# Router of a fuzzy-attention stage on one Trainium2 core: chunks of four batches at the start and of two at the end, shorter lags, late factors on VectorE

## The chip, the cores and the metric

The kernel runs on one core of a Trainium2 chip. The metric is the device time of one execution in microseconds (us), the median of the runs shown. Lower is better.

## What is computed

A two-layer audio model on 32 sequences of 255 tokens with 128 features. The stages are, in order: signature features of the input (L0_tok), fuzzy attention (L0_attn), a top-1 mixture of 8 experts (L0_ffn), relative attention, and a top-2 mixture of 64 experts. The change lies in the fuzzy-attention stage, which also prepares the top-1 experts. Cut to what matters:

```python
# fuzzy attention, added to h
x = layernorm(h)
p = softmax(q @ k.T)
h = h + max(min(p / 0.3, (1 - p) / 0.3), 0) @ x
# top-1 experts: which expert each token goes to
y = layernorm(h)
logits = y @ Wr + br
expert = argmax(logits)          # top_k with k = 1
h = h + ffn[expert](y)
```

## The kernel before, in words

One function, `fuzzy_attention`, holds the stage. Each engine (SyncE, VectorE, ScalarE, GpSimd, TensorE) has its own program, written out by hand as a loop over steps `b`. A step of an engine does pieces of work for batches at fixed offsets from `b`; on VectorE for example the maxima of batch b+2, the membership of b+1, the rows of b+4, the factors of b+2 and then the add of batch b (line 809: the attention result is added to `h`; lines 811 to 813: its statistics). Every engine executes its program strictly in that order, and the engines wait for each other on semaphores that count (`score_done`, `out_done`, `h_ready` and so on). A batch is two tiles of 128 tokens.

Beside the attention runs the router of the next stage. It works on chunks of `G` = 4 batches (`CT` = 8 tiles), N = 8 chunks. For a chunk c:

- **factors** (GpSimd, `factors0`, lines 1018 to 1042): from the batches' statistics the reciprocal deviation `rstd0` and the shift `shift0`, 22 chained small instructions. They wait for the last batch's statistics. GpSimd's program is factors of c, then the sends of chunk c-2, for c = 0 to 9. The last chunk's factors are on VectorE with a square root on ScalarE (`last_factors`, lines 904 to 920; line 1009).
- **normalise** (VectorE, `normalised`, line 824): the chunk's tiles into `y`, in halves of four tiles, at steps 4c+5 and 4c+6.
- **turn rows** (TensorE, `turn_rows`, line 1121) at steps 4c+6 and 4c+8, behind that step's other work, and ScalarE's copy to `yT` (`read_rows`, line 996) at 4c+7 and 4c+9.
- **route** (TensorE, line 1131): the logits, at step 4c+10, and **choose** (VectorE, lines 830 to 852): the expert of each token, at the end of the same step. It gives `both_ready`.
- **count** (TensorE, lines 1142 to 1149) at step 4c+11, ahead of the attention result of that step (line 1112): it needs `both_ready`. **Locate** (VectorE, lines 859 to 870): each token's place in the slots; it gives `at_ready`.
- **send** (GpSimd, line 1053): one indirect DMA per tile scatters the normalised rows to `x_slots` in HBM. Before the sends of tiles 3 and 6 it waits for `out_done` of a later batch.

The chunk N-2 is routed at step 32, after the last batch, with the last chunk behind it. At the end TensorE forms the total count (line 1155), and VectorE's `plan` (lines 873 to 902) writes the table of padding places (line 876) and the tables of the expert stage. SyncE then writes eight blocks of padding rows (lines 758 to 766), each after reading its place from the table. The next stage, `experts_top1`, waits on SyncE for all sends and all padding writes (lines 1239 and 1240) and then loads tiles of `x_slots` (line 1230). `logit_ps` and `count_ps` lie beside the attention result in the two `out_ps` buffers.

```python
for c in range(N + 2):
    if c < N - 1:
        factors0(c)
    if c > 1:
        send(c - 2)
```

Of the kernel before, what the change touches and what calls it, by code (L numbers as in the profile page):

```python
# [8 lines left out]
U32 = mybir.dt.uint32  # L9
# [5 lines left out]
P = 128  # L15
# [6 lines left out]
G = 4  # L22
# [652 lines left out]
NB0, U0, U1 = 5, 8, 8  # L675
ST0 = (B * L + E0 * (P - 1)) // P + 1
# [16 lines left out]
def fuzzy_attention(nc, K, h, mean, rstd, stats, weights, x_slots, no_token, tables, cleared, behind, sent, padded):  # L693
# [5 lines left out]
    CT = 2 * G  # L699
    N = NT // CT  # L700
# [3 lines left out]
    with Bench(nc, "fuz") as m:  # L704
        def ring(name, shape, n=2):
# [11 lines left out]
        logit_ps, count_ps = (out_ps[k][:, 0, D:D + CT * E0].rearrange("p (t e) -> p t e", e=E0) for k in range(2))  # L717
# [23 lines left out]
         total_done, pads_ready, tables_ready, tick_ready, var_ready, std_ready) = (m.sem(n) for n in (  # L741
             "stats_ready vec gp rstd_ready y_ready y_turned yT_ready logit_done both_ready count_done at_ready "
             "total_done pads_ready tables_ready tick_ready var_ready std_ready").split())
        def run(step, ahead):
            for b in range(-ahead, B + 2 * G + 4):
                step(b)
# [6 lines left out]
        def chunk(b, lag, work):  # L753

            if (b - lag) % G == 0 and 0 <= (b - lag) // G < N:
                work((b - lag) // G)

        with nc.Block(no_gpsimd_drain=True) as block:
# [10 lines left out]
            def _(dve):  # L769
# [47 lines left out]
                def normalised(c, k):  # L817

                    n = c % NB
                    dve.wait_ge(rstd_ready, c + 1)  # L820
                    if c >= NB:
                        dve.wait_ge(sent[n], 16 * CT * (c // NB))
                    for t in range(k * G, (k + 1) * G):
                        last = nc.vector.tensor_scalar(y[n][:, t, 0:D], h[:, c * CT + t, :], rstd0[c % 2][:, t:t + 1],
                                                       shift0[c % 2][:, t:t + 1], ALU.mult, ALU.add)
                    last.then_inc(y_ready, 1)

                def choose(c):

                    j = c % 2  # L830
                    rank = K["rank0"][:].unsqueeze(1).to_broadcast(wide)
                    dve.wait_ge(logit_done, c + 1)
                    link(nc.vector.tensor_tensor(logits[:], logit_ps, bias_sb[:].unsqueeze(1).to_broadcast(wide),
                                                 ALU.add))
                    link(nc.vector.tensor_reduce(best[:], logits[:], AX.X, ALU.max))
                    link(nc.vector.tensor_tensor(mask[:], logits[:], best[:].unsqueeze(2).to_broadcast(wide),
                                                 ALU.is_equal))

                    link(nc.vector.tensor_tensor(mask[:], mask[:], rank, ALU.mult))
                    link(nc.vector.tensor_reduce(first[j][:], mask[:], AX.X, ALU.max))  # L840
                    link(nc.vector.tensor_tensor(onehot[j][:], rank, first[j][:].unsqueeze(2).to_broadcast(wide),
                                                 ALU.is_equal))
# [3 lines left out]
                    nc.vector.tensor_tensor(both[j][:], onehot[j][:], K["real"][:, c * CT:(c + 1) * CT].unsqueeze(2)  # L846
                                            .to_broadcast(wide), ALU.mult).then_inc(both_ready, 1)
                    dve.wait_ge(both_ready, c + 1)
                    link(nc.vector.tensor_reduce(chunk_sum[:], both[j][:].rearrange("p t e -> p e t"), AX.X, ALU.add))
# [4 lines left out]
                def locate(c):  # L854

                    j, n = c % 2, c % NB
                    tiles = slice(c * CT, (c + 1) * CT)
                    dve.wait_ge(count_done, c + 1)
                    link(nc.vector.tensor_tensor(mask[:], onehot[j][:], count_ps, ALU.mult))
                    link(nc.vector.tensor_reduce(place[:], mask[:], AX.X, ALU.add))  # L860
                    link(nc.vector.scalar_tensor_tensor(place[:], first[j][:], -float(REGION), place[:],
                                                        ALU.mult, ALU.add))
                    link(nc.vector.scalar_tensor_tensor(place[:], place[:], float(E0 * REGION), K["real"][:, tiles],
                                                        ALU.add, ALU.mult))
                    if c >= NB:
                        dve.wait_ge(sent[n], 16 * CT * (c // NB))
                    nc.vector.tensor_tensor(at[n][:], place[:], K["pad_to"][:, tiles], ALU.add)
                    dve.wait_ge(y_ready, 2 * c + 2)
                    nc.vector.tensor_copy(y[n][:, :, ROW_AT].bitcast(U32), K["pair_row"][:, tiles])\
                        .then_inc(at_ready, 1)  # L870

                def plan(c):

                    dve.wait_ge(total_done, 1)
                    link(nc.vector.tensor_copy(counts[:], count_ps[:, 0, :]))
# [28 lines left out]
                def last_factors():  # L904

                    c = N - 1
                    mean_e, m2_e, mean_o, m2_o = (stats[:, c * CT:NT, k] for k in (1, 2, 4, 5))
                    dve.wait_ge(stats_ready, B)
                    dve.wait_ge(rstd_ready, c)
                    dve.wait_ge(y_ready, 2 * c - 2)  # L910
                    link(nc.vector.tensor_tensor(spread[:], mean_e, mean_o, ALU.subtract))
                    link(nc.vector.scalar_tensor_tensor(spread[:], spread[:], 0.25, spread[:], ALU.mult, ALU.mult))
                    link(nc.vector.tensor_tensor(var[:], m2_e, m2_o, ALU.add))
                    link(nc.vector.scalar_tensor_tensor(var[:], var[:], 1.0 / D, spread[:], ALU.mult, ALU.add))
# [100 lines left out]
            def _(pool):  # L1015
                link = Chain(pool, gp)

                def factors0(c):
# [5 lines left out]
                    if c >= 2:  # L1024
                        pool.wait_ge(y_ready, 2 * c - 2)
# [2057 lines left out]
```

## Time and profile before

| | us |
|---|---|
| Runs | 1925.25, 1920.18, 1919.71 |
| Median | 1920.18 |
| Span of the profiled execution | 1922.3 |

The page gives no time of the profiled execution apart from its span, so the span stands for both. PE is TensorE's matmuls, DVE VectorE, ACT ScalarE, POOL GpSimd, SPq SyncE's queue of DMA issues. PEclk is the clock granted to TensorE, 1.00 for 2.4 GHz and 0.50 for 1.2 GHz. In a timeline a row has the start and the length in us; `x4` means that four like instructions are merged; behind it, in brackets, stands the idle time of the engine before the row and what ended it. `fuz_`, `exp_` and `all_` name the stage of a tile (`all_h` is `h`).

### The profile page before, as it was taken

The numbers are of one execution on the slowest core, as the hardware profiler recorded it, in microseconds if no ns is written. First come the engines' busy times: TensorE is split into PE (matmuls) and PEld (weight loads), VectorE is DVE, ScalarE is ACT, GpSimd is POOL, SyncE is SP. The second block draws the span as 40 slices with busy tenths as digits, with TensorE's granted clock in tenths as the row PEclk, the third lists the DMA queues.
The fourth block names the chain that finished last, engine by engine and source line by source line (L and its number), as shares of the span: only waits on it lengthen the run. The fifth ranks groups of instructions, "written<-read, shape, count | busy, mean of one in ns | idle before, by whom it ended". The sixth has DMA issues, their size and how long they took to land. (4 is left out here: it accounts for less than half of the span.)

```text
span 1922.3 us, 59270 instructions
## 1 busy us (share of the span) xinstructions
PE 1656.3 (86%) x21927; PEld 1392.3 (72%) x21927; DVE 1402.0 (73%) x3369; ACT 938.9 (49%) x2305; POOL 882.1 (46%) x1710
## 2 busy tenths in 40 slices
PE   5999999999979884999599999999999999648750
PEld 4888888888858773999478888888888888525430
DVE  6777777877758884666787888888888888635434
ACT  2222212221228770677467777777777777424320
POOL 3333333333202566566232455445555555547771
PEclk9999999999989995999699999999999999869985
DMA  8900000000022001222323333333333333256537
GB/s 298 165 0 0 0 0 0 0 0 0 0 81 102 23 25 55 65 72 65 124 60 63 74 87 78 77 77 78 76 79 80 86 77 78 63 149 171 169 102 271
DMA packets 312667, 147.60 MB, mean 77 GB/s; under 512 B 205238, under 2 KB 291284, under 8 KB 312020
## 3 DMA queue, kind: packets, MB, share of 16 engines
q1 hardware_dynamic: 299876, 118.38, 25.3%
q0 software_dynamic: 12544, 25.91, 3.9%
q8 instruction: 157, 2.57, 0.6%
q14 instruction: 90, 0.74, 0.1%
HBM read 72.03 MB, written 73.37 MB: 76 GB/s over the span
## 5 line engine op out<-in xcount | busy, mean ns | idle before, releaser
L2143 POOL DMA_INDIRECT x_slots<-rel_x,rel_at x128 | 135.5, 1059 | 212.5 <-PE rel_s_ps L1727 186.9
L535 PE MATMUL tok_main_ps<-tok_w_h,tok_feat_h 128*128 128x512 f32 x512 | 205.3, 401 | 0.9 <-DVE tok_feat_low L99 0.9
L1966 ACT ACTIVATE rel_e<-rel_s_ps,rel_neg_max 128x255 f32<-128x255 f32 x512 | 200.2, 482 | 10.7 <-DVE rel_neg_max L2299 9.5
L535 PE MATMUL tok_main_ps<-tok_w_h,tok_feat_l 128*128 128x512 f32 x512 | 200.6, 392 | 0.0
L535 PE MATMUL tok_main_ps<-tok_w_l,tok_feat_h 128*128 128x512 f32 x512 | 200.3, 391 | 0.0
L2299 DVE TENSOR_REDUCE rel_neg_max<-rel_s_ps 128x4 f32<-128x1020 f32 x128 | 155.9, 1218 | 53.2 <-PE rel_s_ps L1727 51.2
L84 POOL TENSOR_TENSOR tok_q_pre<-tok_v_q,tok_v 128x128 f32 (+1 forms) x32 | 39.0, 1219 | 310.5 <-DVE tok_q L274 295.8
L1707 PE MATMUL rel_s_ps<-rel_k_h,rel_q_head_h 128*128 128x256 f32 x512 | 154.6, 302 | 0.2 <-DVE rel_q_head_l L2273 0.2
L1748 PE MATMUL rel_t_ps<-all_k_ident,rel_e 128*128 128x128 f32 x1024 | 139.3, 279 | 14.4 <-issue 14.0
L294 DVE TENSOR_TENSOR tok_prod<-tok_main_ps,tok_v 128x1024 f32<-128x1024 f32 x64 | 78.4, 1225 | 97.9 <-PE tok_main_ps L540 97.9
L1748 PEld LDWEIGHTS rel_t_ps<-all_k_ident,rel_e 128*128 128x128 f32 x1024 | 109.6, 141 | 47.0 <-issue 45.8
L1707 PE MATMUL rel_s_ps<-rel_k_l,rel_q_head_h 128*128 128x256 f32 x512 | 143.5, 280 | 0.0
L1707 PE MATMUL rel_s_ps<-rel_k_h,rel_q_head_l 128*128 128x256 f32 x512 | 143.2, 280 | 0.0
L2661 POOL DMA_INDIRECT y_rows<-exp_y,exp_x x128 | 123.4, 964 | 34.7 <-issue 33.8
L301 DVE TENSOR_REDUCE tok_inc<-tok_prod 128x128 f32<-128x1024 f32 x64 | 128.1, 2002 | 2.2
L435 ACT ACTIVATE tok_r2v_h<-tok_r2v 128x1024 fp32r<-128x1024 f32 x32 | 33.9, 1061 | 191.6 <-DVE tok_r2v L84 191.6
L1762 PE MATMUL rel_t_ps<-attn_value_table,rel_eT 128*32 128x64 f32 x6656 | 119.5, 221 | 0.8 <-DVE rel_eT L2307 0.7
L1762 PEld LDWEIGHTS rel_t_ps<-attn_value_table,rel_eT 128*32 128x32 f32 x6656 | 98.9, 110 | 24.7 <-issue 20.8
L445 ACT ACTIVATE tok_feat_h<-tok_a_ps 128x512 fp32r<-128x512 f32 x64 | 38.3, 598 | 156.8 <-PE tok_a_ps L521 136.4
L1975 ACT ACTIVATE rel_eT<-rel_t_ps 128x512 f32<-128x512 f32 x128 | 76.5, 598 | 74.9 <-PE rel_t_ps L1748 74.8
L535 PEld LDWEIGHTS tok_main_ps<-tok_w_h,tok_feat_l 128*128 128x128 f32 x512 | 96.5, 189 | 21.0
L535 PEld LDWEIGHTS tok_main_ps<-tok_w_h,tok_feat_h 128*128 128x128 f32 x512 | 97.0, 189 | 19.2 <-DVE tok_feat_low L99 1.0
(406 smaller groups left out, 4725.2 us busy)
## 6 DMA issues: line engine op xcount, KB each, us to landing
rel_q_rep<-q_rows SPq DMA_DIRECT2D x256, 64.0 KB, 2.5
o_rows<-rel_rv SPq DMA_DIRECT2D x256, 64.0 KB
x_slots<-early_zeros SPq DMA_DIRECT2D x16, 520.0 KB, 6.2
exp_x<-x_slots SPq DMA_DIRECT2D x32, 260.0 KB, 3.0
y_rows<-early_zeros SPq DMA_DIRECT2D x16, 512.0 KB, 5.8
final_y<-y_rows SPq DMA_DIRECT2D x16, 512.0 KB, 12.0
exp_x<-x_slots SPq DMA_DIRECT2D x72, 65.0 KB, 1.9
q_rows<-rel_qT SPq DMA_DIRECT2D x64, 64.0 KB
```

Of the source, the lines that this page charges most:

```text
L84: return nc_eng.tensor_tensor(out, left.unsqueeze(3).to_broadcast([P, n, a, c]), right.unsqueeze(2).to_broadcast([P, n, a, c]), ALU.mult)
L294: nc.vector.tensor_tensor(prod[:, s], main_ps[s][:].rearrange("p (c o) -> p c o", c=C), vt[:, bass.ds(2 * b + s, 1), :].rearrange("p n c - ...
L301: nc.vector.tensor_reduce(inc[:, s, :], prod[:, s].rearrange("p c o -> p o c"), AX.X, ALU.add).then_inc(inc_ready, 1)
L535: nc.tensor.matmul(main_ps[s][:, cols], feat[fk][:, s, j, :], w_p[wk][:, j, cols], start=(j == 0 and (fk, wk) == (0, 0)), stop=False)
L1707: nc.tensor.matmul(s_ps[u % 2][:, n, :], q_head[r][qk][:, 4 * blk:4 * blk + 4].rearrange("p c h i -> p (c h i)"), keys_for(k_p[r][kk], u), ...
L1748: last = nc.tensor.transpose(t_ps[:, t, n, :], e[u % 2][:, n, t * P:(t + 1) * P], ident[:])
L1762: last = nc.tensor.matmul(rv_ps[32 * c:32 * c + 32, n, :], eT[s][:, t, blk % (NBLK // 2), 32 * c:32 * c + 32], vtab[:, w:w + QUAD, :].rear ...
L1966: last = nc.scalar.activation(e[u % 2][:, n, 0:L], s_ps[u % 2][:, n, 0:L], ACT.Exp, bias=neg_max[u % 2][:, n:n + 1])
L1975: nc.scalar.activation(eT[s][:, 0, n:n + UB], t_ps[:, 0], ACT.Copy).then_inc(eT_a, 1)
L2143: nc.gpsimd.indirect_dma_start(x1_slots[:], bass.IndirectOffsetOnAxis(ap=at[n][:, k, t:t + 1], axis=0), x1[n][:, t, k, :], None).then_inc( ...
L2299: nc.vector.tensor_reduce(neg_max[u % 2][:], s_ps[u % 2][:, :, 0:L], AX.X, ALU.max, negate=True)\
L2661: nc.gpsimd.indirect_dma_start(y1_rows[:], bass.IndirectOffsetOnAxis(ap=x[j][:, t, ROW_AT:ROW_AT + 1].bitcast(U32), axis=0), y[j][:, t, :] ...
```

## The change

The chunks get sizes of their own: six of four batches and four of two. The pieces of a chunk are placed by functions of the chunk: normalise at `rows_at`, which is the last batch's step + 2 (for chunks 0 to 6) or + 1 (7 to 9); the turned rows one step after it, one half per step, now ahead of route, count and result; route two or three steps after `rows_at`, locate one more. Factors of chunks 7 to 9 move to VectorE, with a Newton iteration in place of ScalarE's square root. The guards of the sends come two batches earlier. `logit_ps` and `count_ps` move to the buffer that belongs to their step.

```diff
+SIZES0 = (4,) * 6 + (2,) * 4
+FIRSTS0 = tuple(sum(SIZES0[:c]) for c in range(len(SIZES0)))
+ON_POOL0 = 7
+def sent_before(c, j=None):
+    j = c % NB0 if j is None else j
+    return 16 * sum(2 * SIZES0[k] for k in range(c) if k % NB0 == j)
...
-            for b in range(-ahead, B + 2 * G + 4):
+            for b in range(-ahead, B + G + 1):
...
-        def chunk(b, lag, work):
-            if (b - lag) % G == 0 and 0 <= (b - lag) // G < N:
-                work((b - lag) // G)
+        def halves(c):
+            return 2 * SIZES0[c] // G
+        def half(c, k=0):
+            return sum(halves(j) for j in range(c)) + k
+        def last_of(c):
+            return FIRSTS0[c] + SIZES0[c] - 1
+        def tiles_of(c):
+            return slice(2 * FIRSTS0[c], 2 * (FIRSTS0[c] + SIZES0[c]))
+        def rows_at(c, k=0):
+            return last_of(c) + (2 if c < ON_POOL0 else 1) + k
+        def route_at(c):
+            return rows_at(c) + 1 + halves(c)
+        def at_step(b, when, work):
+            for c in range(N):
+                if when(c) == b:
+                    work(c)
+        def half_at_step(b, lag, work):
+            for c in range(N):
+                for k in range(halves(c)):
+                    if rows_at(c, k) + lag == b:
+                        work(c, k)
+        def beside(b, s, c):
+            return out_ps[b % 2][:, s, D:D + 2 * SIZES0[c] * E0].rearrange("p (t e) -> p t e", e=E0)
+        def logit_ps(c):
+            return beside(route_at(c), 0, c)
+        def count_ps(c):
+            return beside(route_at(c) + 1, 1, c)
...
-                def last_factors():
-                    c = N - 1
...
+                def late_factors(c):
+                    j, k = c % 2, 2 * SIZES0[c]
...
+                    dve.wait_ge(stats_ready, last_of(c) + 1)
                     dve.wait_ge(rstd_ready, c)
...
+                    dve.wait_ge(y_ready, half(c - 1))
+                    link(nc.vector.tensor_tensor(center_c, mean_e, mean_o, ALU.add))
+                    link(nc.vector.tensor_tensor(spread_c, mean_e, mean_o, ALU.subtract))
+                    link(nc.vector.scalar_tensor_tensor(spread_c, spread_c, 0.25, spread_c, ALU.mult, ALU.mult))
+                    link(nc.vector.tensor_tensor(var_c, m2_e, m2_o, ALU.add))
+                    link(nc.vector.tensor_scalar(var_c, var_c, 1.0 / D, EPS, ALU.mult, ALU.add))
+                    link(nc.vector.tensor_tensor(var_c, var_c, spread_c, ALU.add))
+                    link(nc.vector.tensor_scalar(root_c.bitcast(I32), var_c.bitcast(I32), -0.5, float(0x5f3759df),
+                                                 ALU.mult, ALU.add))
+                    for i in range(3):
+                        link(nc.vector.tensor_tensor(newton_c, root_c, root_c, ALU.mult))
+                        link(nc.vector.scalar_tensor_tensor(newton_c, newton_c, -0.5, var_c, ALU.mult, ALU.mult))
+                        link(nc.vector.scalar_tensor_tensor(root_c if i < 2 else rstd0[j][:, 0:k], newton_c, 1.5, root_c,
+                                                            ALU.add, ALU.mult))
+                    nc.vector.scalar_tensor_tensor(shift0[j][:, 0:k], center_c, -0.5, rstd0[j][:, 0:k],
+                                                   ALU.mult, ALU.mult).then_inc(rstd_ready, 1)
...
-                    if b == B:
-                        last_factors()
-                        choose(N - 2)
-                        locate(N - 2)
-                    chunk(b, 5, lambda c: normalised(c, 0))
-                    chunk(b, 6, lambda c: normalised(c, 1))
-                    chunk(b, 10, lambda c: c == N - 2 or choose(c))
-                    chunk(b, 11, lambda c: c == N - 2 or locate(c))
+                    at_step(b, lambda c: route_at(c) + 1, locate)
+                    at_step(b, rows_at, lambda c: c < ON_POOL0 or late_factors(c))
+                    half_at_step(b, 0, normalised)
+                    at_step(b, route_at, choose)
...
-                    chunk(b, 7, lambda c: read_rows(c, 0))
-                    chunk(b, 9, lambda c: c == N - 2 or read_rows(c, 1))
-                    if b == B:
-                        read_rows(N - 2, 1)
-                        act.wait_ge(var_ready, 1)
-                        nc.scalar.activation(var[:], var[:], ACT.Sqrt).then_inc(std_ready, 1)
+                    half_at_step(b, 1, read_rows)
...
-                    pool.wait_ge(stats_ready, (c + 1) * G)
+                    pool.wait_ge(stats_ready, last_of(c) + 1)
+                    if c >= 1:
+                        pool.wait_ge(rstd_ready, c)
...
-                    for t in range(CT):
-                        if t in (3, 6):
-                            pool.wait_ge(out_done, min(G * (c + 2) + 5 + t // 3, B))
+                    for t in range(2 * SIZES0[c]):
+                        if t in (3, 6) and last_of(c) + 8 + t // 3 < B:
+                            pool.wait_ge(out_done, last_of(c) + 8 + t // 3)
...
-                    if c < N - 1:
+                    if c < ON_POOL0:
                         factors0(c)
...
                 def route(c):
-                    pe.wait_ge(yT_ready, 2 * c + 2)
-                    pe.wait_ge(h_ready, min(G * c + 9, B))
+                    pe.wait_ge(yT_ready, half(c + 1))
+                    pe.wait_ge(h_ready, min(route_at(c) - 1, B))
                     if c >= 1:
                         pe.wait_ge(both_ready, c)
...
                     pe.wait_ge(both_ready, c + 1)
-                    pe.wait_ge(h_ready, min(G * c + 10, B))
+                    pe.wait_ge(h_ready, min(route_at(c), B))
...
                     on(b + 3, project)
-                    chunk(b, 10, lambda c: c == N - 2 or route(c))
-                    chunk(b, 11, lambda c: c == N - 2 or count(c))
+                    half_at_step(b, 1, turn_rows)
+                    at_step(b, route_at, route)
+                    at_step(b, lambda c: route_at(c) + 1, count)
                     on(b, result)
                     on(b + 1, turn_f)
                     on(b + 4, turn)
-                    chunk(b, 6, lambda c: turn_rows(c, 0))
-                    chunk(b, 8, lambda c: turn_rows(c, 1))
-                    if b == B:
-                        route(N - 2)
-                        count(N - 2)
```

In the other hunks the chunk's slices take the chunk's own size.

## Rows read from the trace of the kernel before

**Rows 1.** The page: the profiled execution's span

```profile
span 1922.3 us, 59270 instructions
```

**Rows 2.** Stretches: us, busy us (count) by engine, TensorE clock, DMA

```profile
680.00:700.00 20.00, 18.11 (x123) 14.94 (x122) 17.26 (x65) 15.10 (x44) 12.89 (x32) 1.00 0.09 29
...
722.00:726.00 4.00, 4.00 (x20) 3.96 (x20) 1.28 (x5) 0.46 (x1) 3.09 (x4) 0.50 0.15 50
726.00:730.00 4.00, 1.91 (x17) 1.55 (x16) 2.62 (x13) 0.74 (x2) 2.13 (x3) 0.50 0.16 50
770.00:775.00 5.00, 4.12 (x18) 3.83 (x19) 1.04 (x3) 1.74 (x6) 0.00 (x0) 0.50 0.24 56
```

**Rows 3.** POOL's timeline, 700 to 785 us: start, length, line, instruction

```profile
707.09 0.95 POOL L1053 DMA_INDIRECT x_slots<-fuz_y,fuz_at_u  x1 [0.30 <-issue]
710.93 0.20 POOL L1026 TENSOR_TENSOR fuz_center<-all_stats 128x8 f32<-128x8 f32 x1 [2.89 <-DVE all_stats L812]
...
717.42 0.23 POOL L1042 TENSOR_SCALAR fuz_shift<-fuz_center 128x8 f32<-128x8 f32 x1
...
763.78 0.96 POOL L1053 DMA_INDIRECT x_slots<-fuz_y,fuz_at_u  x1 [0.31 <-issue]
```

**Rows 4.** DVE's timeline, 655 to 703 us

```profile
670.09 0.42 DVE L809 TENSOR_TENSOR all_h<-all_h,fuz_out_ps 128x256 f32<-128x256 f32 x1
...
689.99 0.42 DVE L809 TENSOR_TENSOR all_h<-all_h,fuz_out_ps 128x256 f32<-128x256 f32 x1
```

**Rows 5.** DVE's timeline, 700 to 775 us

```profile
705.34 0.21 DVE L833 TENSOR_TENSOR fuz_logits<-fuz_out_ps,all_gate_bias 128x64 f32<-128x64 f32 x1
...
706.97 0.22 DVE L846 TENSOR_TENSOR fuz_both<-fuz_onehot,all_k_real 128x64 bf16<-128x64 f32 x1
...
709.90 0.42 DVE L809 TENSOR_TENSOR all_h<-all_h,fuz_out_ps 128x256 f32<-128x256 f32 x1
...
710.76 0.20 DVE L859 TENSOR_TENSOR fuz_mask<-fuz_onehot,fuz_out_ps 128x64 f32<-128x64 f32 x1
...
711.83 0.68 DVE L781 TENSOR_REDUCE fuz_neg_max<-fuz_score_ps 128x2 f32<-128x510 f32 x1
...
718.43 1.10 DVE L824 TENSOR_SCALAR fuz_y<-all_h,fuz_rstd,fuz_shift 128x128 f32<-128x128 f32 x4
...
730.93 0.42 DVE L809 TENSOR_TENSOR all_h<-all_h,fuz_out_ps 128x256 f32<-128x256 f32 x1 [2.03 <-PE fuz_out_ps L1112]
...
732.83 0.17 DVE L911 TENSOR_TENSOR fuz_spread<-all_stats 128x8 f32<-128x8 f32 x1
733.03 0.17 DVE L912 SCALAR_TENSOR_TENSOR fuz_spread<-fuz_spread 128x8 f32<-128x8 f32 x1
...
748.09 0.22 DVE L833 TENSOR_TENSOR fuz_logits<-fuz_out_ps,all_gate_bias 128x64 f32<-128x64 f32 x1 [6.32 <-PE fuz_out_ps L1131]
...
752.34 0.17 DVE L876 TENSOR_TENSOR moe_pad_at<-fuz_counts,all_k_region 128x8 uint32<-128x8 f32 x1
```

**Rows 6.** PE's timeline, 700 to 785 us

```profile
719.81 2.93 PE L1131 MATMUL fuz_out_ps<-all_gate,fuz_yT 128*128 128x8 f32 x16 [2.11 <-ACT fuz_yT L996]
722.60 2.06 PE L1112 MATMUL fuz_out_ps<-fuz_x,fuz_fT 128*128 128x128 f32 x8
...
725.30 1.06 PE L1121 MATMUL fuz_route_ps<-all_k_ident,fuz_y 128*128 128x128 f32 x4
728.45 0.23 PE L1142 MATMUL fuz_out_ps<-fuz_both,all_k_after_b 128*128 128x64 bf16 x1 [2.09 <-DVE fuz_both L846]
...
732.37 3.58 PE L1131 MATMUL fuz_out_ps<-all_gate,fuz_yT 128*128 128x8 f32 x16 [0.69 <-ACT fuz_yT L996]
```

**Rows 7.** SP's timeline, 740 to 785 us

```profile
753.59 9.93 SPq L766 DMA_DIRECT2D x_slots<-in_no_token  x8
768.34 16.82 SPq L1230 DMA_DIRECT2D exp_x<-x_slots  x11
```

**Rows 8.** SP's waits, 740 to 790 us: us in total, times, longest

```profile
SPq L1239 <- DMA x_slots<-fuz_y,fuz_at_u: 2.1, 1, 2.1
```

More of the change, by code:

```diff
@@ L698, in fuzzy_attention @@
     U = 8
[L699 to L700 removed]
+    CT = 2 * max(SIZES0)
+    N = len(SIZES0)
     NB = NB0
@@ L1020, in factors0 @@
                     j = c % 2
-                    tiles = slice(c * CT, (c + 1) * CT)
+                    tiles, n = tiles_of(c), 2 * SIZES0[c]
                     mean_e, m2_e, mean_o, m2_o = (stats[:, tiles, k] for k in (1, 2, 4, 5))
-                    pool.wait_ge(stats_ready, (c + 1) * G)
+                    center_c, spread_c, var_c, root_c, newton_c = (t[:, 0:n] for t in (center, spread, var, root, newton))
+                    pool.wait_ge(stats_ready, last_of(c) + 1)
+                    if c >= 1:
+                        pool.wait_ge(rstd_ready, c)
@@ L1031, in factors0 @@
-                    link(nc.gpsimd.tensor_scalar(var[:], var[:], 1.0 / D, None, ALU.mult))
-                    link(nc.gpsimd.tensor_tensor(var[:], var[:], spread[:], ALU.add))
-                    link(nc.gpsimd.tensor_scalar(root[:].bitcast(I32), var[:].bitcast(I32), -0.5, float(0x5f3759df),
+                        pool.wait_ge(y_ready, half(c - 1))
+                    link(nc.gpsimd.tensor_tensor(center_c, mean_e, mean_o, ALU.add))
+                    link(nc.gpsimd.tensor_tensor(spread_c, mean_e, mean_o, ALU.subtract))
@@ L1105, in result @@
                     pe.wait_ge(fT_ready, b + 1)
-                    chunk(b, 12, lambda c: pe.wait_ge(both_ready, c + 1))
-                    chunk(b, 13, lambda c: pe.wait_ge(at_ready, c + 1))
+                    at_step(b - 2, route_at, lambda c: pe.wait_ge(both_ready, c + 1))
+                    at_step(b - 3, route_at, lambda c: pe.wait_ge(at_ready, c + 1))
                     if b >= 2:
@@ L1124, in route @@
                 def route(c):
-                    pe.wait_ge(yT_ready, 2 * c + 2)
-                    pe.wait_ge(h_ready, min(G * c + 9, B))
+                    pe.wait_ge(yT_ready, half(c + 1))
+                    pe.wait_ge(h_ready, min(route_at(c) - 1, B))
                     if c >= 1:
                         pe.wait_ge(both_ready, c)
-                    for t in range(CT):
-                        last = nc.tensor.matmul(logit_ps[:, t, :], yT[t // G][:, t % G, :], gate_sb[:],
+                    for t in range(2 * SIZES0[c]):
+                        last = nc.tensor.matmul(logit_ps(c)[:, t, :], yT[half(c, t // G) % 2][:, t % G, :], gate_sb[:],
                                                 start=True, stop=True)
```

125 lines of the change are left out of this document (58 added, 67 removed).

## The prediction

> **What bounds the kernel now.** I began at the page: one core, a span of 1922.3 us [rows 1]. The chain that ended last stays in the last expert stage, so it says nothing of this change. Stages follow each other, so what counts is when the next stage can start. I then cut the fuzzy-attention stage into stretches [rows 2]: in its steady part TensorE is busy 18.11 of 20 us and VectorE 17.26, at full clock; from 722 us on the clock stands at 0.50 of full. Numbered adds (line 809, one per batch) date the steps: add(19) at 670.09, add(23) at 689.99 [rows 4], so four batches take 19.90 us; add(27) at 709.90 and add(31), the last, at 730.93 [rows 5].
>
> GpSimd's timeline shows the end: its sends (line 1053) take 0.96 us each with 0.30 between, the last 24 of them stand back to back from about 734, and the last starts at 763.78 and ends at 764.74 [rows 3]. SyncE then waits 2.1 us for that transfer [rows 8] and issues the next stage's first load at 768.34 [rows 7]. That load is my mark: what moves it moves the rest. Close behind lie the eight padding writes, issued from 753.59 to 763.52 [rows 7], after VectorE wrote their table at 752.34 to 752.51 [rows 5].
>
> **The change, on the last steps.** Written out from the diff, the last five chunks are: 5 (batches 20 to 23), 6 (24, 25), 7 (26, 27), 8 (28, 29), 9 (30, 31). VectorE's steps become: step 27: add(27), normalise 6. Step 28: add, factors of 7, normalise 7, choose 5. Step 29: add, locate 5, choose 6. Step 30: add, locate 6, factors of 8, normalise 8, choose 7. Step 31: add, locate 7. Then factors of 9, normalise 9, choose 8, locate 8, choose 9, locate 9. TensorE's: step 28: turn rows of 6, route 5, result(28). Step 29: turn 7, route 6, count 5, result(29). Step 30: route 7, count 6, result(30). Step 31: turn 8, count 7, result(31). Both engines work in order. So from step 29 on each result stands behind a count that waits for both_ready, which VectorE gives only at the end of its step before. That loop is the heart of my forecast.
>
> **Prices.** Add with its statistics 0.86 us (709.90 to 710.76), locate 1.07 (710.76 to 711.83), choose until both_ready 1.85 (705.34 to 707.19), four tiles normalised 1.01 longer of engine time inside the 1.10 shown, one small chained instruction 0.20 (732.83 to 733.03) [rows 5]. Halved chunks save little: an instruction on 128x64 takes 0.22 and one on 128x8 takes 0.17 [rows 5], so one on 128x32 lies between; I take 1.65 for choose and 1.00 for locate. The late factors are 17 chained instructions: 17 x 0.203 = 3.45 us. Their integer-typed one has no row on VectorE; the 0.17 us rows and twice that bound it, which is 0.2 us. On TensorE at half clock: four transposes 1.06, route of eight tiles 3.58 and so of four 1.79, a result 2.06 [rows 6]; count and result together until the add, 728.45 [rows 6] to 730.93 [rows 5], 2.48.
>
> **Steady part.** Chunks 0 to 5 hold the same instructions, on other batches: still 19.9 us per four batches. Locate and normalise now share a step where choose and normalise did; I allow 0.2 us per period, 1.3 in all (ends -1 and +3). Add(27) then starts at 711.2. The sends' guards move with it and cost nothing, hidden by GpSimd's idle 2.89 us per period [rows 3].
>
> **Step 27.** GpSimd runs factors 5, send 3, factors 6 in order. Send 3 ended at 708.04, 709.3 now. Factors took 710.93 to 717.65, 22 instructions, 6.7 us [rows 3]; with 0.3 between, those of chunk 6 are ready at 716.4 (half-size operands save nothing I can show). VectorE wants them at 711.2 + 0.86 = 712.1: it stands 4.3 us, with the maxima of batch 30 queued behind it. Before, factors 6 were not wanted until 718.43. Chunk 6 is normalised at 717.5. TensorE, whose turn of these rows stands before route 5 and result(28), idles too.
>
> **Step 28.** In the trace before, TensorE idled 2.11 us before 719.81 [rows 6] and the clock was 0.50 after it [rows 2]. The new idle is about 4 us, so I take half clock from here. Turn 0.9, route 5 3.5, result 2.06 and hand-over: 6.5 us, add(28) at 724.0.
>
> **Step 29.** 0.86 + 3.45 + 1.01 + 1.85 = 7.17, then route 6 (it waits for the same both_ready, and stands ahead) 1.79, count and result 2.48: add(29) 11.4 later, 735.4.
>
> **Step 30.** 0.86 + 1.07 + 1.65 + 1.79 + 2.48 = 7.85: add(30) at 743.3.
>
> **Step 31.** 0.86 + 1.00 + 3.45 + 1.01 + 1.65 + 2.48 = 10.45: add(31) at 753.8. Before, it was 730.93: 22.9 us later.
>
> **After the last add.** Add 0.86, locate 7 1.00, factors 9 3.45, normalise 1.01, choose 8 1.65: 761.8. Count 8 and route 9, 2.3: 764.1. From choose of the last chunk to the padding table it was 748.09 to 752.51, 4.4 us [rows 5]; the small chunk saves 0.3: 768.2. This part takes 14.4 us where 21.6 stood (730.93 to 752.51), so it does what it is meant to. The waits added to GpSimd's factors (for the earlier factors' semaphore) are met by its own order and cost nothing. The removed square root's round trip to ScalarE and the second wait for turned rows lie in this saving.
>
> **The end.** Chunk 9's four sends start near 767.8 and end near 774 with queue time: no longer last. The padding writes are: 1.08 to the first, 9.93 for eight, ending at 779.2. From there to the first load: at least the 3.60 seen after the last send less the 2.1 waited, 1.5, at most 3.6 [rows 7, 8]; I take 2.4, nearer the middle since a landing must still be waited for. First load at 781.6 against 768.34: **13.3 us later**. VectorE's plan (7 us after the table) stays hidden under the padding writes, as before. The code of later stages and their work is untouched, and shifts one for one.
>
> Sum, against the profiled execution: 1922.3 + 13.3 = 1935.6. That execution is 2.1 above the median 1920.18, so I predict 1933.5. The terms together: +1.3 steady, +21.6 in steps 28 to 31, -7.2 after the last add, -2.4 because the padding writes close a gap behind the sends that used to be the end.
>
> **The rivals.**
>
> Rival 1, TensorE keeps or regains its full clock. TensorE's terms above add to 6.5 + 4.3 + 4.3 + 2.5 + 2.3 = 19.9 us at half clock; at full clock about 9 of it goes. First load +4, time 1924.5. For it: if chunk 6's factors come in time, there is no idle to lose the clock in; and in step 28 TensorE works some 8 us unbroken. Against: between 722 and 726 it was busy 4.00 of 4.00 at 0.50, and the next stretch still showed 0.50; at 770 to 775 it was busy 4.12 of 5 at 0.50 [rows 2]. The Trainium skill, "TensorE: Matmul & The Clock Gate", Part 1, says that sustained work brings the clock back to full; by it step 28 would end at full clock, yet the waits of steps 29 to 31 would lose it again, so it would give a time between the two, about 1930. A clock regained in part is, from the rows alone, half of the 9 us, first load +9: I give that 0.15 inside the forecast's 0.64. Rival 1 itself: chance 0.18.
>
> Rival 2, faster: the late chains fit into idle time. For it: from 722 to 730 VectorE is busy only 1.28 + 2.62 of 8 us [rows 2]. If steps 28 to 31 kept their pace, add(31) would come at 732.2, the table 14.4 later at 746.6, the padding writes' end at 757.6, the first load at 760.0: 8.3 us earlier, 1912. The point that decides is count 5 in TensorE's step 29: if both_ready(5) is there before fT(29), this holds. Against: the chain is on VectorE between add(28) and both_ready(5), 7.2 us, and the idle time it would fill is itself a wait for TensorE. Chance 0.10.
>
> Rival 3, no change: chunk 6's wait is absent and the three factor chains cost half, by an overlap I don't see; 4.3 and some 5 us less, first load +4 or less, 1920 to 1924. Chance 0.06, as VectorE's chained 0.20 us is measured.
>
> **How the numbers follow.** The forecast has 0.64, range 1928 to 1937.5 (steady -2 and +2, clock partly back -4, first load 1.5 to 3.6 after the padding). The remaining 0.02 is slower still. The range that should hold 8 in 10 takes in most of rival 1 and 3: 1921.5 to 1937.5. A difference of 0.3%, 5.8 us, is about what a measurement of this kernel can tell from no change; so slower begins at 1926. Slower: the forecast 0.64, a third of rival 1, and what lies above, 0.73. Same: the rest of rivals 1 and 3, 0.16. Faster: 0.11.
>
> **What would show it.** In the changed kernel's trace: VectorE waits about 4 us for GpSimd before line 824's tiles near 712; adds 27 to 31 are some 42 us apart in all, not 21, with TensorE's counts (line 1142 before) each waiting over 5 us for both_ready; granted clock 0.5 from about 717; from the last add to the padding table about 14 us; sends end before the padding writes. If the adds of steps 28 to 31 stay 4 to 7 us apart, I am wrong, and rival 2 or 3 holds. If three of the four gaps stay near 9.5 (7.17 + 0.9 + 1.4 for step 29, with TensorE's terms halved) at full clock, rival 1 does.

## The result and the profile after

The changed kernel takes 1937.43 us (median of 4 runs, 1936.59 to 1939.23) against 1920.2 (4 runs beside it, 1919.71 to 1925.25): a ratio of 1.0078, interval 1.006 to 1.0096. The interval lies above 1, so the changed kernel is slower, by under 1%. The profiled execution took 1938.27 us with a span of 1936.5, where the one of before had a span of 1922.3 [rows 1].

VectorE's timeline of the changed kernel, 700 to 790 us (line 856 is now the add, line 871 the normalising, lines 962 to 975 the late factors, line 896 gives `both_ready`):

```profile
708.99 0.42 DVE L856 TENSOR_TENSOR all_h<-all_h,fuz_out_ps 128x256 f32<-128x256 f32 x1
709.45 0.49 DVE L859 BATCH_NORM_STATS2 all_stats<-all_h 128x6 f32<-128x128 f32 x2
713.63 1.12 DVE L871 TENSOR_SCALAR fuz_y<-all_h,fuz_rstd,fuz_shift 128x128 f32<-128x128 f32 x4 [3.70 <-POOL fuz_shift L1092]
...
721.08 0.42 DVE L856 TENSOR_TENSOR all_h<-all_h,fuz_out_ps 128x256 f32<-128x256 f32 x1 [4.28 <-PE fuz_out_ps L1162]
...
721.94 0.18 DVE L962 TENSOR_TENSOR fuz_center<-all_stats 128x4 f32<-128x4 f32 x1
...
723.15 0.24 DVE L968 TENSOR_SCALAR fuz_root<-fuz_var 128x4 int32<-128x4 int32 x1
...
725.20 0.16 DVE L975 SCALAR_TENSOR_TENSOR fuz_shift<-fuz_center,fuz_rstd 128x4 f32<-128x4 f32 x1
725.39 1.12 DVE L871 TENSOR_SCALAR fuz_y<-all_h,fuz_rstd,fuz_shift 128x128 f32<-128x128 f32 x4
...
728.04 0.21 DVE L896 TENSOR_TENSOR fuz_both<-fuz_onehot,all_k_real 128x64 bf16<-128x64 f32 x1
...
732.50 0.42 DVE L856 TENSOR_TENSOR all_h<-all_h,fuz_out_ps 128x256 f32<-128x256 f32 x1 [1.57 <-PE fuz_out_ps L1162]
...
740.08 0.42 DVE L856 TENSOR_TENSOR all_h<-all_h,fuz_out_ps 128x256 f32<-128x256 f32 x1 [2.72 <-PE fuz_out_ps L1162]
...
750.48 0.42 DVE L856 TENSOR_TENSOR all_h<-all_h,fuz_out_ps 128x256 f32<-128x256 f32 x1 [1.95 <-PE fuz_out_ps L1162]
...
764.41 0.17 DVE L926 TENSOR_TENSOR moe_pad_at<-fuz_counts,all_k_region 128x8 uint32<-128x8 f32 x1
```

The adds 27 to 31 stand at 708.99, 721.08, 732.50, 740.08 and 750.48: 41.49 us, where before they stood 21.02 apart [rows 5]. VectorE waits 3.70 us for chunk 6's factors behind add(27). Of the chain of 17 small instructions the first starts at 721.94 and the last ends at 725.36; the integer-typed one is line 968, 0.24 us. The padding table is at 764.41 to 764.58.

GpSimd's timeline, 704 to 780 us, tells why those factors are late: they start when send 3 is out (its last DMA 706.09 to 707.04) and take until 713.60. The sends of chunk 9 end at 771.75.

```profile
706.09 0.95 POOL L1103 DMA_INDIRECT x_slots<-fuz_y,fuz_at_u  x1 [0.30 <-issue]
707.07 0.21 POOL L1076 TENSOR_TENSOR fuz_center<-all_stats 128x4 f32<-128x4 f32 x1
...
713.37 0.23 POOL L1092 TENSOR_SCALAR fuz_shift<-fuz_center 128x4 f32<-128x4 f32 x1
...
714.12 1.08 POOL L1103 DMA_INDIRECT x_slots<-fuz_y,fuz_at_u  x1 [0.36 <-issue]
...
770.79 0.96 POOL L1103 DMA_INDIRECT x_slots<-fuz_y,fuz_at_u  x1 [0.30 <-issue]
```

TensorE's timeline, 700 to 780 us (line 1171 turns rows, 1181 routes, 1192 counts, 1162 is the attention result):

```profile
714.81 1.12 PE L1171 MATMUL fuz_route_ps<-all_k_ident,fuz_y 128*128 128x128 f32 x4 [3.26 <-DVE fuz_y L871]
715.72 3.42 PE L1181 MATMUL fuz_out_ps<-all_gate,fuz_yT 128*128 128x8 f32 x16
718.99 2.05 PE L1162 MATMUL fuz_out_ps<-fuz_x,fuz_fT 128*128 128x128 f32 x8
...
726.57 1.11 PE L1171 MATMUL fuz_route_ps<-all_k_ident,fuz_y 128*128 128x128 f32 x4 [2.97 <-DVE fuz_y L871]
728.40 1.85 PE L1181 MATMUL fuz_out_ps<-all_gate,fuz_yT 128*128 128x8 f32 x8 [0.72 <-DVE fuz_both L896]
730.10 0.21 PE L1192 MATMUL fuz_out_ps<-fuz_both,all_k_after_b 128*128 128x64 bf16 x1
...
730.41 2.05 PE L1162 MATMUL fuz_out_ps<-fuz_x,fuz_fT 128*128 128x128 f32 x8
...
736.15 1.84 PE L1181 MATMUL fuz_out_ps<-all_gate,fuz_yT 128*128 128x8 f32 x8 [2.84 <-DVE fuz_both L896]
...
746.61 1.12 PE L1171 MATMUL fuz_route_ps<-all_k_ident,fuz_y 128*128 128x128 f32 x4 [5.71 <-DVE fuz_y L871]
```

In every step from 28 on TensorE waits for VectorE: 3.26 us in step 28, 2.97 and 0.72 in step 29, 2.84 in step 30, 5.71 in step 31. The stretches of the changed kernel (us, busy us by engine, TensorE clock, DMA), which answer to [rows 2]:

```profile
710.00:714.00 4.00, 1.54 (x7) 0.75 (x5) 0.37 (x2) 1.33 (x4) 2.76 (x14) 1.00 0.01 2
714.00:718.00 4.00, 3.19 (x16) 3.20 (x16) 2.47 (x8) 2.62 (x8) 3.11 (x3) 0.52 0.10 33
718.00:722.00 4.00, 4.00 (x19) 4.00 (x19) 0.88 (x4) 0.17 (x2) 2.95 (x4) 0.50 0.15 50
722.00:726.00 4.00, 1.60 (x4) 0.70 (x3) 3.41 (x21) 1.02 (x2) 1.84 (x2) 0.50 0.18 54
...
738.00:742.00 4.00, 2.89 (x17) 2.49 (x14) 1.75 (x10) 0.60 (x1) 2.98 (x4) 0.57 0.15 50
742.00:750.00 8.00, 3.00 (x17) 2.60 (x18) 5.67 (x31) 0.60 (x1) 6.29 (x8) 0.68 0.18 57
750.00:760.00 10.00, 4.61 (x26) 4.03 (x25) 8.21 (x46) 0.60 (x1) 4.60 (x6) 0.50 0.10 34
```

The clock is still full in the idle stretch from 710 to 714 and is at half behind it. Single microseconds show where it came back: 0.50 up to 741, then full while TensorE has no work at all, and 0.50 again from 745, ahead of its next row at 746.61.

```profile
742.00:743.00 1.00, 0.00 (x0) 0.00 (x0) 0.83 (x6) 0.00 (x0) 0.86 (x1) 1.00 0.21 67
743.00:744.00 1.00, 0.00 (x0) 0.00 (x0) 0.83 (x6) 0.00 (x0) 0.83 (x1) 1.00 0.21 67
```

SyncE's timeline, 740 to 790 us, which answers to [rows 7]:

```profile
765.65 9.90 SPq L813 DMA_DIRECT2D x_slots<-in_no_token  x8
777.95 8.48 SPq L1276 DMA_DIRECT2D exp_x<-x_slots  x8
```

The padding writes are now what ends last: their issues end at 775.55, and the next stage's first load comes 2.40 later.

### The profile page after: what moved, and what is told of

The parts are those of the page before. It is cut to its first block and busy times, and to the rows that moved or that the text cites. A ratio compares the mean times of both kernels' runs of the same rounds, so it can differ in the third digit from the quotient of the medians.

```text
span 1936.5 us, 59363 instructions
## 1 busy us (share of the span) xinstructions
PE 1665.7 (86%) x21929; PEld 1396.7 (72%) x21929; DVE 1413.4 (73%) x3444; ACT 939.3 (49%) x2304; POOL 883.6 (46%) x1712
```

## The experiments

All stage times below come from profiled executions, from one mark to the next. The four numbers ahead of "31 to table" are the gaps between the starts of the adds of batches 27, 28, 29, 30 and 31; the table's mark is the end of the instruction that writes it; "27 to load" is the whole, from add(27) to the next stage's first load.

| kernel | gaps | 31 to table | table to load | 27 to load | median us (ratio, interval) |
|---|---|---|---|---|---|
| before, first | 3.98, 3.69, 7.12, 6.24 | 21.58 | 15.83 | 58.44 | |
| before, e9 | 3.98, 3.69, 5.23, 6.34 | 19.97 | 15.75 | 54.96 | 1925.40 (0.9995, 0.9982 to 1.0009) |
| before, e11 | 3.98, 3.69, 5.57, 6.24 | 21.61 | 14.44 | 55.53 | one run, 1923.78 |
| before, e12 | 3.98, 3.69, 5.62, 6.24 | 21.60 | 14.42 | 55.55 | one run, 1923.21 |
| changed | 12.09, 11.42, 7.57, 10.40 | 14.09 | 13.38 | 68.96 | 1937.43 (1.0078, 1.006 to 1.0096) |
| changed, e5 | 12.09, 11.43, 7.58, 10.41 | 14.11 | 13.35 | 68.97 | 1939.93 (1.0073, 1.0056 to 1.009) |
| changed, e10 | 12.09, 11.42, 7.58, 10.40 | 14.11 | 13.42 | 69.02 | 1942.36 (1.0096, 1.0077 to 1.0115) |
| e1 factors early | 5.83, 11.43, 6.77, 10.36 | 14.27 | 13.38 | 62.04 | 1930.22 (1.0036, 1.0019 to 1.0054) |
| e2 six Newton | 12.06, 13.35, 7.14, 12.31 | 15.88 | 13.38 | 74.12 | 1942.39 (1.0091, 1.0072 to 1.0111) |
| e3 all fours | 5.38, 5.28, 5.94, 4.91 | 19.95 | 13.91 | 55.38 | 1923.17 (0.9991, 0.9978 to 1.0003) |
| e4 keep clock | 9.01, 9.85, 5.84, 10.35 | 13.63 | 13.49 | 62.18 | 1935.61 (1.006, 1.0043 to 1.0077) |
| e6 route wait | 12.07, 10.36, 5.95, 10.30 | 14.12 | 13.37 | 66.16 | 1937.53 (1.0076, 1.0053 to 1.01) |
| e7 off the loop | 5.55, 9.77, 6.18, 8.45 | 18.29 | 13.25 | 61.50 | 1930.04 (1.0035, 1.0022 to 1.0048) |
| e8 fours, turned last | 3.92, 5.40, 5.78, 3.05 | 20.05 | 14.50 | 52.70 | 1921.89 (0.9982, 0.9972 to 0.9992) |

The ratios are against runs of the kernel before on the same chip, whose medians were 1924.01 (e1 to e4), 1924.95 (e5 to e8) and 1926.21 (e9, e10). The medians follow the stage only roughly. e2's lies 18.4 us above the kernel before, where the unaltered changed kernel's lie 15.0 to 17.2 above it, though e2's stage is 5.2 longer; e6's is 2.4 below that of e5 on the same chip, with four runs that span 12 us. So what an experiment says of a single wait rests on its profiled execution.

**e1: chunk 6's factors ahead of send 3's second half.** GpSimd computes them after four of the eight sends of chunk 3.

```diff
 # in send(), behind the indirect DMA of tile t
+if c == 3 and t == 3:
+    factors0(6)
 # in GpSimd's loop over c
-if c < ON_POOL0:
+if c < ON_POOL0 and c != 6:
     factors0(c)
```

> Chunk 6's factors come after four of chunk 3's sends on GpSimd instead of after all eight. My theory: VectorE no longer waits 3.70 us for them in step 27, so add(28) comes some 3.7 us sooner after add(27) (8.4 us or less instead of 12.1), and since TensorE then has almost no idle time there, its clock stays up at least through step 28, which saves up to 3 us more; steps 29 to 31 stay near 11.4, 7.8 and 10.4 us. From add(27) to the first load 65 us or less, where the changed kernel has 68.96 and the kernel before 58.44. Rival: the wait was idle time that the later steps would have had anyway, then 69 us. Rival: with the clock kept for good, 57 to 60.

VectorE no longer waits there. In e1's timeline of VectorE, 705 to 730 us, the adds 27 and 28 stand 5.83 apart, where the changed kernel has 12.09:

```profile
711.35 0.42 DVE L856 TENSOR_TENSOR all_h<-all_h,fuz_out_ps 128x256 f32<-128x256 f32 x1
...
717.18 0.42 DVE L856 TENSOR_TENSOR all_h<-all_h,fuz_out_ps 128x256 f32<-128x256 f32 x1 [1.82 <-PE fuz_out_ps L1164]
```

The whole falls from 68.96 to 62.04, by 6.9 us: 6.26 of it in the first gap and 0.80 in the third, less 0.18 behind the last add. The wait itself was 3.70; the rest of the first gap, 2.6, is step 28's TensorE work at full clock:

```profile
714.00:718.00 4.00, 4.00 (x35) 3.95 (x35) 1.81 (x7) 3.04 (x9) 3.21 (x5) 1.00 0.20 63
```

The 0.80 of the third gap is clock as well: e1's route 7 takes 1.03 us at 732.27, with the clock at 1.00 in 730 to 733, where the changed kernel's takes 1.84. So a 3.7 us wait cost 6.9.

**e2: six Newton rounds in the late factors in place of three.** The values are the same to rounding; only the length of the chain is changed.

```diff
-for i in range(3):
+for i in range(6):
 ...            # the last round is i == 5 in place of i == 2
```

> The Newton iteration of the late factors on VectorE runs six rounds in place of three: nine more chained instructions of 0.20 us, 1.8 us for each of chunks 7, 8 and 9. My theory: all three chains lie on the path, so step 29 takes 1.8 us more (13.2), step 31 1.8 more (12.2) and the stretch from add(31) to the padding table 1.8 more (15.9); from add(27) to the first load 74.4 us, 5.4 more than the changed kernel. Rival: the chains run in time that is waited for anyway, then no step grows and it stays at 69.

Nine more instructions of 0.20 us are 1.8 us per chain. The second gap grew by 1.93, the fourth by 1.91, the part behind the last add by 1.79; the whole by 5.16. Each of the three late chains lies on the path with its full length. The third gap gave back 0.43, and TensorE's clock was at 1.00 from 737 to 739 there.

**e3: eight chunks of four, with all the rest of the change.**

```diff
-SIZES0 = (4,) * 6 + (2,) * 4
+SIZES0 = (4,) * 8
```

> The chunks are eight of four batches again; the shorter lags, the placing of the pieces and the late factors on VectorE stay. My theory: it is the four small chunks that load steps 28 to 31, so add(27) to add(31) takes 22 to 24 us in place of 41.5, the table comes 20 to 21 us after add(31), and the last chunk's eight sends end it: first load 55.5 to 58 us after add(27), as in the kernel before (58.44) or 1 to 3 us sooner. Rival: the shorter lags themselves are what costs, then it stays over 64 us.

27 to load is 55.38, within what the kernel before shows, and the ratio's interval holds 1. The shorter lags by themselves cost nothing and bring nothing; the whole loss comes with the four small chunks. Their two further chains of factors on VectorE come with them: in e3 only the last chunk has its factors there, as in the kernel before. Small chunks with factors on GpSimd were not run, so what the halving costs without those chains stays open.

**e4: TensorE kept busy.** Unused transposes fill TensorE's waits; the rest is the changed kernel.

```diff
+def busy(n):
+    for _ in range(n):
+        nc.tensor.transpose(turn_ps[:, 1, 0:P], ident[:], ident[:])
 on(b + 3, project)
+busy({28: 30, 29: 30, 30: 28, 31: 44, 33: 40, 35: 16}.get(b, 0))
```

> TensorE transposes the identity into an unused half of a PSUM bank while it would be idle: 30, 30, 28, 44, 40 and 16 times in steps 28, 29, 30, 31, 33 and 35. Nothing reads it. My theory: the granted clock stays at 1.00 from 712 to 760 us; TensorE's terms halve, step 28 takes 9 to 10 us (12.1), step 29 9.6 (11.4), step 30 6 to 6.5 (7.6), step 31 9.4 (10.4), and from add(27) to the first load it is 61 to 64 us in place of 69. Rival: the time hangs on VectorE's chain alone and the clock is only seen beside it; then the steps keep their lengths, 68 to 70 us. If the clock falls all the same, the added transposes take twice their time and the steps grow by 1 to 3 us each.

e4's stretches show the clock at 1.00 in all from 710 to 742 (two of the eight are shown) and at 0.57 from 742 to 750; the changed kernel had 0.50 to 0.57 from 714 to 742:

```profile
714.00:718.00 4.00, 4.00 (x40) 4.00 (x38) 2.84 (x9) 1.81 (x7) 2.94 (x6) 1.00 0.07 24
718.00:722.00 4.00, 4.00 (x34) 3.85 (x34) 2.32 (x12) 2.00 (x4) 3.08 (x4) 1.00 0.18 59
...
742.00:750.00 8.00, 7.09 (x40) 6.95 (x39) 5.22 (x30) 0.60 (x1) 5.88 (x9) 0.57 0.17 52
```

27 to load is 62.18, so half clock costs at least 6.8 us. It is no price for all four steps: the clock still fell to 0.50 from 743 to 749, in step 31, where the result took 2.04 us again and the gap did not shrink (10.35 against 10.40). The loop stays: 35.05 us for the four gaps. The profiled run took 1930.59 us, but the nine runs lie between 1927.87 and 1939.96 and their median is 1935.61. The granted clock over a whole run was 0.950 to 0.953 in the three fastest and 0.945 to 0.949 in the others. That would fit a clock that was kept for less of this stage, but only one execution was profiled, so the 6.8 us hold for that one.

**e5, e10: the changed kernel again; e9, e11, e12: the kernel before again.** No edit.

> The changed kernel, unaltered, beside the kernel before on one chip. The medians first measured lie 17.2 us apart, the two profiles' mark (the first load of the next stage) only 9.6. My theory: the router's stage costs 11.8 us (27.0 us from add(27) on reckoned to the load: 68.96 against 58.44, and 1.3 before it), and the rest of the 17.2 is scatter of what lies before and behind it, which differs from one execution to the next by up to 5 us; so here the difference of medians is 10 to 14 us, and from the first load to the end it takes 1154 to 1160 us as in all profiles so far. Rival: the change also slows a later stage by some 5 us; then the difference is 16 to 18 and the part after the first load is 1158 or more.

> The kernel before, unaltered, in another profile. Its first profile had 1153.9 us from the first load to the end, the changed kernel's two 1158.5 and 1159.9. My theory: that part scatters by itself; here it is anywhere from 1153 to 1161 us, the stage itself repeats to 0.3 us (add(27) to the first load 58.4), and the ratio is 1.000. Rival: the part after the router is really shorter in the kernel before, then it is 1154 us again, within 1.

> The changed kernel once more on the same chip. Router 68.9 to 69.0 us from add(27) to the first load; from there to the end 1153 to 1161 us by my theory, 1158 or more by the rival that a later stage is slower too. Difference of the medians 10 to 15 us.

> The kernel before, unaltered, one more profiled execution. Two executions of it are at hand: from add(27) to the first load 58.44 us in one and 54.96 us in the other, of the same instructions. If the shorter course is the usual one, this shows 54.5 to 55.5 us and a load-to-end time near 1156.7; then the stage of the changed kernel (69.0 us in three executions) costs 14, and nothing of the medians' difference of 15 to 17 us has to be looked for elsewhere but 1 to 3. If the longer one is usual, it shows 58 to 59, and 3 to 5 us stay unexplained.

> The same as for the run ahead of it: add(27) to the first load 54.5 to 55.5 us if the shorter course is the usual one, 58 to 59 if the longer is.

The changed kernel's stage repeats to 0.06 us. Three expectations missed: the differences of the medians are 15.0 (e5) and 16.2 us (e10), not 10 to 14 and 10 to 15, and the kernel before's stage does not repeat to 0.3 us (e9): the execution from which I predicted, with 58.44, is the longest of four, the others have 54.96, 55.53 and 55.55. The difference lies in the gap from add(29) to add(30), and in the step from the last send to the load, 3.60 there and 2.20 to 2.21 in the others. In e9 the table comes 1.6 earlier too, since the route behind add(31) takes 1.95 us there and 3.58 in the first execution; but the sends end the stage. The clock makes the difference in that gap: in e11 route and result of step 30 take 1.95 and 1.48 us, in the first execution 2.93 and 2.06, which is the 1.55 between their third gaps. e9's stretches show the clock full from 718 to 722, where the first execution had already lost part of it and then stood at 0.50 [rows 2], and partly back at 726 to 734. What lengthened the step from the last send to the load is not shown.

```profile
718.00:722.00 4.00, 2.75 (x24) 2.75 (x25) 1.75 (x6) 1.20 (x3) 3.24 (x3) 1.00 0.12 37
722.00:726.00 4.00, 1.86 (x10) 1.46 (x9) 3.50 (x15) 1.19 (x2) 2.93 (x4) 0.51 0.15 50
726.00:730.00 4.00, 3.21 (x22) 2.95 (x22) 1.79 (x9) 0.74 (x2) 1.86 (x2) 0.63 0.16 52
730.00:734.00 4.00, 1.85 (x16) 1.75 (x16) 3.32 (x21) 1.35 (x2) 2.18 (x4) 0.79 0.05 17
```

**e6: route without the wait for a buffer that it doesn't share.** Route waits for `both_ready` of the chunk before it only where both have their logits in the same buffer.

```diff
-pe.wait_ge(both_ready, c)
+pe.wait_ge(both_ready, c if (route_at(c) - route_at(c - 1)) % 2 == 0 else c - 1)
```

> In the changed kernel, route of a chunk whose logits go to the other PSUM buffer than those of the chunk before waits for the choice one chunk earlier: chunks 6 and 7. My theory: route 6 and route 7 then run before both_ready of chunks 5 and 6 and leave the path, each 1.8 us at half clock: step 29 takes 9.6 us (11.4), step 30 5.9 (7.6), and from add(27) to the first load 65.5 us (68.96). Rival: VectorE, whose next piece is the add, holds them anyway, or route 6 waits for its rows' copy on ScalarE instead; then 68 to 69.

e6's TensorE timeline, 705 to 765 us: route 6 follows turn 7 at once, and route 7 waits 1.18 us for ScalarE's copy of the rows, no longer 2.84 for VectorE.

```profile
727.73 1.72 PE L1181 MATMUL fuz_out_ps<-all_gate,fuz_yT 128*128 128x8 f32 x8
...
733.69 1.88 PE L1181 MATMUL fuz_out_ps<-all_gate,fuz_yT 128*128 128x8 f32 x8 [1.18 <-ACT fuz_yT L1048]
```

The second gap lost 1.06 and the third 1.62, the whole 2.8; I had expected 1.8 for each and 65.5 for the whole. The count behind it still waits for the same semaphore.

**e7: all of it off the loop.** e1 and e6 together; VectorE chooses before it computes late factors and normalises; TensorE turns rows at the end of its step.

```diff
 # VectorE
+at_step(b, route_at, choose)
 at_step(b, rows_at, lambda c: c < ON_POOL0 or late_factors(c))
 half_at_step(b, 0, normalised)
-at_step(b, route_at, choose)
 # TensorE
-half_at_step(b, 1, turn_rows)
 ...
 on(b + 4, turn)
+half_at_step(b, 1, turn_rows)
```

> Every wait that I name is taken out of the loop of steps 28 to 31, with the small chunks kept: chunk 6's factors early (as in the first experiment), the route's wait relaxed, VectorE chooses before it computes the late factors and normalises, and TensorE turns rows at the end of its step. My theory: what is left is VectorE's own work, 9.8, 5.8, 9.3 us in steps 28 to 30, so the gaps from add(27) on are about 5.8 to 6.4, 9.6, 6.0, 8.6, 30 us in all, and from add(27) to the first load it is 58.5 to 61.5: still no faster than the kernel before (58.44). Rival: it was waiting, not work; then the adds come 21 to 24 us apart in all and the load 52 to 55 us after add(27).

27 to load is 61.50, little better than e1 alone. The four gaps take 29.95, but the part behind the last add is 18.29, 4.2 longer: what was taken out of the steps comes back there. e7's VectorE timeline, 710 to 765 us, has only these waits of over 0.2 us before 755:

```profile
714.60 0.17 DVE L837 RECIPROCAL fuz_inv<-fuz_total 128x2 f32<-128x2 f32 x1 [0.30 <-ACT fuz_e L1008]
...
716.48 0.42 DVE L856 TENSOR_TENSOR all_h<-all_h,fuz_out_ps 128x256 f32<-128x256 f32 x1 [1.51 <-PE fuz_out_ps L1164]
...
725.97 0.17 DVE L837 RECIPROCAL fuz_inv<-fuz_total 128x2 f32<-128x2 f32 x1 [0.30 <-ACT fuz_e L1008]
...
732.43 0.42 DVE L856 TENSOR_TENSOR all_h<-all_h,fuz_out_ps 128x256 f32<-128x256 f32 x1 [1.31 <-PE fuz_out_ps L1164]
...
744.74 0.19 DVE L883 TENSOR_TENSOR fuz_logits<-fuz_out_ps,all_gate_bias 128x32 f32<-128x32 f32 x1 [1.70 <-PE fuz_out_ps L1183]
```

They are 5.12 us in all, 3.42 of it ahead of add(31). The rest of the four gaps, 26.5 us, is VectorE's own work, and that alone is longer than the kernel before's 19.2 to 21.0.

**e8: eight chunks of four, the last one's lag shorter.** e3 with e6's route wait, rows turned at the end of the step, chunk 7 normalised one step after its last batch and chunk 5 three.

```diff
-return last_of(c) + (2 if c < ON_POOL0 else 1) + k
+return last_of(c) + (1 if c == 7 else 3 if c == 5 else 2) + k
```

> Eight chunks of four with the shorter lags (chunk 5 one step later), rows turned at the end of TensorE's step and the relaxed wait of route: the version that I expect to be the fastest. From add(27) to the first load 52 to 55 us, where the kernel before has 58.44 and all fours with the change's order 55.38; the whole kernel 2 to 6 us faster than before, 0.999 to 0.997. Rival: the last chunk's eight sends bound it whatever the order, then 55 to 56.

27 to load is 52.70, 2.3 less than the best of the kernel before, and the ratio is 0.9982 with its interval below 1: 3.1 us faster in the medians, 12 runs against 23. That is less than the 0.3% which I took as the least that a comparison can tell, so it is a small gain seen on one chip. Which of the three alterations to e3 brings it was not tested one by one. Its GpSimd timeline, 712 to 765 us, says what bounds it:

```profile
718.01 1.08 POOL L1103 DMA_INDIRECT x_slots<-fuz_y,fuz_at_u  x1 [0.35 <-issue]
...
759.01 0.96 POOL L1103 DMA_INDIRECT x_slots<-fuz_y,fuz_at_u  x1 [0.31 <-issue]
```

Between these two lie 30 more sends, each issued 1.26 to 1.84 us after the one before. The 32 sends of the last four chunks fill GpSimd from 718.01 to 759.97, and the load follows at 762.23.

## Why the prediction was right, point by point

**Step 27.** Forecast a stall of 4.3 us for chunk 6's factors behind send 3, measured 3.70. Send 3 ended 1.95 ahead of add(27), where I had 1.9. The term was 0.6 too large because the factors began 0.03 behind the send, where I had allowed 0.3, and took 6.5, not 6.7. e1 shows the cause.

**Step 28 and the clock.** I took half clock from there because TensorE would idle; the rows show 1.00 while it idles and 0.52 behind it. Forecast 12.8 for the gap, measured 12.09. From 714.81 to 723.60 TensorE then worked without a break, and the clock stood at 0.50 in every microsecond from 715 to 724; the result took 2.05 us, as it does at half clock, and not 1.06. In the part of rival 1 in which the clock comes back by halves, it comes back for the work of steps 29 to 31. It did not: it was back from 741 to 745 only, averaged to 0.57 and 0.68 in the two stretches above, and TensorE stood idle in just these microseconds. By the Trainium skill, "TensorE: Matmul & The Clock Gate", Part 1, sustained work would have brought it to full at the end of step 28; the trace doesn't agree.

**Steps 29 to 31, the loop.** Forecast 11.4, 7.85 and 10.45, measured 11.42, 7.57 and 10.40. TensorE's result stands behind a route or a count that waits for VectorE, and VectorE's next add stands behind that result. e2 shows that the loop passes on the length of the chain one for one, e6 that the route's wait is one turn of it. The forecast in my list that the counts would wait over 5 us each was wrong: in steps 29 and 30 route stands ahead and takes the wait (0.72 and 2.84), and of step 31's 5.71 it is the turn of rows, for VectorE's normalising, that waits. The waits are on the same chain, under other lines.

**The chain's price.** 17 x 0.203 = 3.45 forecast; from 721.94 to the next instruction at 725.39 it is 3.45. Halved tiles save little, as taken: choose until `both_ready` was put at 1.65, and from 746.47 to the end of line 896 it is 1.6. The Trainium skill, "VectorE: DVE Perf Modes", "The TRN2 errata", gives the reason as a fixed cost per instruction that small tiles pay each time; these durations fit that, 0.16 us for 4 elements a partition and 0.22 for 64 [rows 5].

**After the last add and the end.** Forecast 14.4, then 13.4 to the load; measured 14.09 and 13.38. The padding writes are last, as forecast, and the landing of 2.4 us was right.

**The sum.** Forecast 70.4 from add(27) to the load, measured 68.96. Against the execution that I read, the cost was 10.5 there and 1.31 in the steady part, 11.8, where I had 13.3. Two things beside my terms turned out otherwise. First, the steady part's +1.3 is right by luck. It matched a number that isn't the change's: add(0) to add(27) is 127.27 to 127.30 in the changed kernel and 125.96, 126.78, 127.42 and 127.55 in four executions of the one before. Second, 58.44 was too long a base. Against the mean of the four (56.1) the last part costs 12.9; and from add(0) to the load the mean of before is 183.05, of the changed kernel 196.27: +13.2, which is my sum by errors that cancel. One slip had no effect: I set the span of 1922.3 against the median of the times and called it 2.1 above. A time is longer than its span (1938.27 and 1936.5 in the changed kernel), so that distance was larger, but the forecast is the median plus 13.3 either way.

**From the stage to the total.** I predicted 1933.5 and 1921.5 to 1937.5; 1937.43 lies at the upper edge, and that it fell inside by 0.07 us is luck. The medians differ by 17.2, 15.0 and 16.2 us, each more than my 13.3. Means of four profiled executions of before and three of the changed kernel give: add(0) 1.0 earlier, add(0) to the load 13.2 longer, load to end 2.9 longer (1154.0 to 1156.7 before, 1156.8 to 1160.0 after), 15.1 in all. The 2.9 behind the load, in code that is the same, is the term that I had wrong: I had put it at zero ("shifts one for one"). The other kernels lie from 1153.4 (e7) to 1161.4 (e8) there, so it is no plain cost of this change; what sets it stays open.

**The rivals.** Rival 1 (clock kept) fell. e4 prices it with the clock at full in three of the four steps: 6.8 us, where I had about 9 for all of them, and 62.18 still lies above all of before. Rival 2 (faster) fails at the point it named: fT(29) is there at 722.53, when ScalarE's copy ends, but `both_ready`(5) comes at 728.25; TensorE needs it for route 6, and result(29) starts at 730.41. e7 shows that it fails also with the waits out, since VectorE's own work fills the steps. Rival 3 is e1's case for the first wait (62.04) and is refuted by e2 for the chains. In the chances one sum is off by a little: the parts I listed for slower add up to 0.72, for same to 0.18 and for faster to 0.10, where I wrote 0.73, 0.16 and 0.11.

## What to carry to other kernels

Where two in-order engines hand work back and forth every step, an operation put on one of them is hidden only while its idle time isn't itself a wait for the other; look at who waits for what, not at the busy share. Splitting work into smaller pieces to shorten a tail pays the fixed price of every piece inside the loop ahead of that tail: here 7.5 us were saved behind the last add and 20.5 paid before it (22 against the other executions of the kernel before). And take the base from more than one profiled execution, since one part of this stage differed by 3.5 us between executions of one kernel.

## What the runs showed of the hardware that I had not expected

A wait of 3.70 us on VectorE cost 6.9 with what it did to TensorE's clock. The clock stayed at half through 8.8 us of unbroken work (714.81 to 723.60), and came back once, from 741 to 745, when TensorE had nothing to do. Unused transposes held the clock: in e4's TensorE timeline, 709 to 724 us, 30 of them take 3.44 us and the clock stays at 1.00.

```profile
712.78 3.44 PE L1210 MATMUL fuz_turn_ps<-all_k_ident 128*128 128x128 f32 x30
...
716.49 1.85 PE L1181 MATMUL fuz_out_ps<-all_gate,fuz_yT 128*128 128x8 f32 x16
```

The Trainium skill, "TensorE: Matmul & The Clock Gate", Part 4, says that transposes don't count as work for the clock as other matmuls do. Here these did: with them the clock kept at 1.00 where the changed kernel had lost it by 715. The profile lists them as MATMUL and doesn't show whether TensorE's transpose mode, of which the page speaks, was on.
